# Softplus sum on TensorE, dt*u on VectorE, and three scan inputs in one VectorE instruction

## The reference, cut to what matters

```python
seq = xw.reshape(b, 64, 64).transpose(0, 2, 1)      # 64 steps of one window
x, z = jnp.split(seq @ W_in, 2, axis=-1)            # 128 channels each
x = _silu(conv(x) + conv_b)                         # u
dt, Bm, Cm = jnp.split(x @ W_xproj, [4, 20], axis=-1)
dt = jax.nn.softplus(dt @ W_dt + b_dt)
A = -jnp.exp(A_log)                                 # 128 x 16
def step(h, inp):                                   # h: 128 x 16 states
    h = jnp.exp(dt_t[:, :, None] * A) * h + (dt_t * u_t)[:, :, None] * B_t[:, None, :]
    y = jnp.einsum('bdn,bn->bd', h, C_t)
y = (ys + u * Dp) * _silu(z)
out = y @ W_out
```

## Time and profile before

| | us |
|---|---|
| median of 3 runs (lowest, highest) | 8791.29 (8777.52, 8808.5) |
| the profiled execution | 8805.53 |
| its span in the trace | 8803.7 |
| VectorE busy over the span | 6682.1 (76%) |
| GpSimd busy | 5536.3 (63%) |
| TensorE busy (matmul) | 6314.4 (72%) |
| ScalarE busy | 4408.5 (50%) |
| mean granted clock of TensorE | 0.794 of full speed |

### The profile page before, as it was taken

The page is one execution under the profiler, slowest core; times in us unless marked ns, Lnnn a source line. Parts: engine busy times, 40 slices in busy tenths (PEclk is TensorE's granted clock), DMA queues, the critical chain, the costliest instruction groups (busy, mean ns, idle before and its releaser), DMA issues. The chain is left out here.

```text
span 8803.7 us, 102835 instructions
## 1 busy us (share of the span) xinstructions
PE 6314.4 (72%) x30290; PEld 2534.8 (29%) x30290; DVE 6682.1 (76%) x7810; ACT 4408.5 (50%) x5988; POOL 5536.3 (63%) x2731
## 2 busy tenths in 40 slices
PE   5888888888885767667777766677776766776555
PEld 3444444444442222222222222222222222222133
DVE  3555555555555999999999999999999999999634
ACT  1222222222223766666666666666666667676400
POOL 0000000000004999999999999999999999999600
PEclk8887787787877888887788888887788888788666
DMA  1111111111113555555555555555556555555553
GB/s 30 42 38 42 36 42 38 38 43 36 38 40 115 193 195 198 187 207 185 208 183 205 186 201 194 195 199 192 201 183 210 183 204 186 203 191 197 152 151 128
DMA packets 513971, 1253.45 MB, mean 142 GB/s; under 512 B 170085, under 2 KB 172297, under 8 KB 513673
## 3 DMA queue, kind: packets, MB, share of 16 engines
q1 hardware_dynamic: 513417, 1252.41, 42.2%
q0 software_dynamic: 512, 0.53, 0.0%
HBM read 943.30 MB, written 231.21 MB: 133 GB/s over the span
## 5 line engine op out<-in xcount | busy, mean ns | idle before, releaser
L1177 DVE TENSOR_TENSOR_SCAN b_h<-b_a,b_h 128x448 f32<-128x448 f32 x3584 | 3677.3, 1074 | 294.0 <-POOL b_h L1002 148.2
L1014 POOL TENSOR_TENSOR b_h<-b_h,b_ct 128x896 f32<-128x896 f32 x1792 | 3692.1, 2090 | 24.2 <-DVE b_h L1177 16.6
L1105 ACT ACTIVATE b_a<-b_dts,decay 128x441 f32<-128x441 f32 x3584 | 2227.4, 629 | 1583.9 <-DVE b_h L1177 1564.3
L1264 PE MATMUL b_b<-b_rows,spread_b 16*128 16x512 f32 (+1 forms) x1792 | 697.9, 786 | 1487.5 <-DVE b_h L1167 1486.5
L1025 POOL MEMSET b_seq<- 128x938 f32 x2 | 1.7, 882 | 2645.9 <-POOLq L789 2645.9
L1167 DVE TENSOR_TENSOR b_h<-b_dus,b_b 128x896 f32<-128x896 f32 x1344 | 1432.9, 1066 | 73.7 <-DMA b_dus<-d_dtu 71.3
L490 DVE TENSOR_TENSOR a_xg<-a_xd,a_pb 128x784 f32<-128x784 f32 x512 | 495.3, 967 | 637.7 <-PE a_pb L604 635.5
L1272 PE MATMUL b_y<-b_h,fold 128*32 128x512 f32 (+1 forms) x7168 | 953.7, 659 | 6.8 <-POOL b_h L1014 6.8
L1002 POOL TENSOR_TENSOR b_h<-b_dus,b_bt 128x896 f32<-128x896 f32 x448 | 936.5, 2091 | 10.5 <-DMA b_dus<-d_dtu 10.5
L1264 PEld LDWEIGHTS b_b<-b_rows,spread_b 16*128 16x128 f32 x1792 | 167.4, 228 | 1756.4 <-DVE b_h L1167 1754.7
L1233 PE MATMUL b_w<-b_seq,w_conv 128*128 128x384 f32 (+1 forms) x896 | 540.5, 765 | 12.5 <-DMA b_seq<-b_seq 12.5
(11 more groups left out here) (208 smaller groups left out, 8940.3 us busy)
## 6 DMA issues: line engine op xcount, KB each, us to landing
b_bt<-d_rows SPq DMA_DIRECT2D x448, 448.0 KB, 6.0
b_ct<-d_rows SPq DMA_DIRECT2D x448, 448.0 KB, 3.6
b_dts<-d_dt SPq DMA_DIRECT2D x448, 448.0 KB, 6.0
b_dus<-d_dtu SPq DMA_DIRECT2D x448, 448.0 KB, 6.0
a_xd<-a_xn SPq DMA_DIRECT2D x256, 196.0 KB, 3.4
d_dt<-b_dt SPq DMA_DIRECT2D x112, 448.0 KB, 2.6
d_dtu<-b_soft SPq DMA_DIRECT2D x112, 448.0 KB, 2.5
b_seq<-b_seq SPq DMA_DIRECT2D x112, 234.0 KB, 3.5
```

Source lines behind the costliest of these rows:

```text
L1014: nc.gpsimd.tensor_tensor(hh[t][:], hh[t][:], ct[t // 4 % 2][:], ALU.mult).then_inc(hc_done, 1)
L1105: a(steps(bank(aa, k)), steps(half(dts[t % 4], k)), ACT.Exp, scale=decay[:, t % 4, t // 4:t // 4 + 1]).then_inc(a_done, 1)
L1177: v.tensor_tensor_scan(half(hh[t], k), bank(aa, k), half(hh[t], k), 0.0, ALU.mult, ALU.add).then_inc(h_done, 1)
L1264: last = mm(bb[:, lo:hi], spread_b[q, row, :], rows[i][q, lo:hi], start=True, stop=True)
```

## The change

The sum of softplus leaves POOL. TensorE multiplies `dtb` (relu) and then `soft` (ln) by the identity matrix into `ww`, accumulating; DVE makes `soft` = `ww` * u (`dt_input`, behind the scan of tile 9); ACT copies `ww` into `dtb` (`dt_move`, behind the exps of tile 10). The list has an entry "dt" more, between "xp" and "z". POOL's two products are gone. `softplus_end` is split: Exp at t = 6, Ln at t = 7. `z` moves from t = 10 to 12, the logits from 12 to 14, the tokens from 14 to 15, `residual` from 14 to 15, and POOL's input of the next unit's row 0 from 13 to 14.

The inputs of the three tiles of a row that DVE makes become one instruction of 3 x 896 elements, with `bb` read three times by a stride of zero. It stands at t = 1, 5, 9, 13. `b_done` now counts rows, so TensorE may overwrite `bb` once that one instruction is done. SP stores dt last of the three stores, and loads `dus[1..3]` together behind the input of row 3, ahead of the loads of `dts`.

```diff
-            EVEN = ("xc", "var", "conv", "pre", "xp", "z", "out")
-            ODD = ("xc2", "var2", "conv", "pre", "xp", "z", "lgp", "tok")
+            EVEN = ("xc", "var", "conv", "pre", "xp", "dt", "z", "out")
+            ODD = ("xc2", "var2", "conv", "pre", "xp", "dt", "z", "lgp", "tok")
@@ sync
                             if more:
-                                store_dt(par, o)
                                 sp.wait_ge(moved, spot(i, "xp", it, kind) + 2)
                                 store_rows(par)
                                 store_dtu(par, o)
+                                store_dt(par, spot(i, "dt", it, kind))
...
+                                sp.wait_ge(b_done, row_no(i, 3, it))
+                                for b in range(1, 4):
+                                    load_dus(b, par)
                                 for b in range(4):
                                     sp.wait_ge(a_done, half_no(i, 12 + b, 1, it))
                                     if b == 0:
                                         sp.wait_ge(dt_stored[par], stored)
                                     load_dts(b, par)
-                                    if b:
-                                        sp.wait_ge(b_done, b_no(i, 12 + b, it))
-                                        load_dus(b, par)
@@ gpsimd
-                            nc.gpsimd.tensor_tensor(dtb[:], dtb[:], soft[:], ALU.add).then_inc(dt_ready, 1)
-                            pool.wait_ge(dt_ready, o)
-                            nc.gpsimd.tensor_tensor(soft[:], dtb[:], u[j][:], ALU.mult).then_inc(dtu_ready, 1)
...
-                                if t in (13, 15) and more:
+                                if t in (14, 15) and more:
                                     inputs(1 - i, t // 15, it + i)
@@ scalar
+                        def dt_move(c, o):
+                            act.wait_ge(dtu_ready, o)
+                            move(c, dtb[:])
...
                                 if t == 6 and more:
-                                    softplus_end(o + 1)
+                                    softplus_exp(o + 1)
+                                if t == 7 and more:
+                                    softplus_ln(o + 1)
...
                                 if t == 10 and more:
+                                    dt_move(spot(i, "dt", it, kind), o + 1)
+                                if t == 12 and more:
                                     act.wait_ge(yz_ready, o - 1)
                                     move(spot(i, "z", it, kind), gate[1 - i][:])
-                                if t == 12 and finals:
+                                if t == 14 and finals:
...
-                                if t == 14 and finals:
+                                if t == 15 and finals:
@@ vector
+                        def inputs(row, i, it):
+                            if row == 0:
+                                for b in range(1, 4):
+                                    dve.wait_ge(dus_in[b], 16 * unit_no(i, it))
+                            dve.wait_ge(bt_spread, row_no(i, row, it))
+                            dve.wait_ge(folded, row_no(i, row, it) - 4)
+                            v.tensor_tensor(hh_all[:, 4 * row + 1:4 * row + 4, :], dus_all[:, 1:4, :],
+                                            bb[:, 0:TB].unsqueeze(1).broadcast_to([P, 3, TB]), ALU.mult).then_inc(b_done, 1)
...
+                        def dt_input(c, j, o):
+                            dve.wait_ge(made, c + 2)
+                            v.tensor_tensor(soft[:], ww[:, 0:TB], u[j][:], ALU.mult).then_inc(dtu_ready, 1)
...
-                                if t % 4:
-                                    inputs(t, i, it)
+                                if t % 4 == 1:
+                                    inputs(t // 4, i, it)
...
+                                if t == 10 and not (kind == LAST and i == 1):
+                                    dt_input(spot(i, "dt", it, kind), 1 - i, unit_no(i, it) + 1)
-                                if t == 14 and i == 0 and kind != FIRST:
+                                if t == 15 and i == 0 and kind != FIRST:
@@ tensor
+                        def softplus_sum(c, o):
+                            pe.wait_ge(l_ready, o)
+                            pe.wait_ge(moved, c + 1)
+                            for lo, hi in banks(TB):
+                                mm(ww[:, lo:hi], ident[:], dtb[:, lo:hi], start=True, stop=False)
+                                last = mm(ww[:, lo:hi], ident[:], soft[:, lo:hi], start=False, stop=True)
+                            last.then_inc(made, 1)
...
                             fold_row(0, tile_no(i, 3, it))
                             if more:
+                                softplus_sum(spot(i, "dt", it, kind), unit_no(i, it) + 1)
+                            spread_row(3, i, it)
+                            if more:
                                 gate_in(spot(i, "z", it, kind), 1 - i)
-                            spread_row(3, i, it)
```

More of the change, by code:

```diff
@@ L765, in phase_b @@
                 dts = ring("dts", 4)
-                dus = ring("dus", 4)
+                dus_all = sb("dus", [P, 4, TB])
+                dus = [dus_all[:, n, :] for n in range(4)]
                 bt = ring("bt", 2)
                 ct = ring("ct", 2)
-                hh = ring("h", HH)
+                hh_all = sb("h", [P, HH, TB])
+                hh = [hh_all[:, n, :] for n in range(HH)]
                 aa = psum("b_a", [P, 2 * BANK], F32, st)
@@ L782, in phase_b @@
                 sq_ready, rstd_ready, xn_ready, seq_ready = (sem(n) for n in ("sq", "rstd", "xn", "seq"))
-                abs_ready, e_ready, l_ready, dt_ready, dtu_ready = (sem(n) for n in ("abs", "e", "l", "dt", "dtu"))
+                abs_ready, e_ready, l_ready, dtu_ready = (sem(n) for n in ("abs", "e", "l", "dtu"))
                 skip_ready, yz_ready, gate_ready = (sem(n) for n in ("skip", "yz", "gate"))
                 a_done, h_done = (sem(n, 2 * TILES) for n in ("a", "h"))
-                b_done, hc_done = sem("b", TILES - 8), sem("hc", TILES)
-                pb_done, bt_spread, folded = (sem(n, 8) for n in ("pb", "spread", "fold"))
+                hc_done = sem("hc", TILES)
+                b_done, pb_done, bt_spread, folded = (sem(n, 8) for n in ("b", "pb", "spread", "fold"))
                 sq2_ready, rstd2_ready, xl_ready = (sem(n) for n in ("sq2", "rstd2", "xl"))
@@ L863, in store_rows, with store_dt @@
                             sp.dma_start(rows_d[par, :, :], rows[par][0:2 * NS, :]).then_inc(rows_stored[par], 16)
-                        def store_dt(par, o):
-                            sp.wait_ge(dt_ready, o)
+                        def store_dt(par, c):
+                            sp.wait_ge(moved, c + 2)
                             sp.dma_start(dt_d[par, :, :], dtb[:]).then_inc(dt_stored[par], 16)
@@ L940, in _ @@
                         store_dtu(0, 2)
+                        store_dt(0, START.index("dt"))
                         sp.wait_ge(rows_stored[0], 16)
@@ L1014, in unit @@
                                 nc.gpsimd.tensor_tensor(hh[t][:], hh[t][:], ct[t // 4 % 2][:], ALU.mult).then_inc(hc_done, 1)
-                                if t == 6 and more:
-                                    products(1 - i, unit_no(i, it) + 1)
                                 if t == 4 and i == 0 and kind != LAST:
@@ L1028, in _ @@
                         sequences(None, 1, None)
-                        products(0, 2)
                         inputs(0, 0, 1)
@@ L1144, in _ @@
                         softplus_start(START.index("pre"))
-                        softplus_end(2)
+                        softplus_exp(2)
+                        softplus_ln(2)
                         move(START.index("xp"), rows[0][:], rows=4 * NS)
+                        dt_move(START.index("dt"), 2)
                         act.wait_ge(aa_zero, 1)
@@ L1158, in _ @@
                         v = nc.vector
[L1160 to L1167, removed]
+                        def inputs(row, i, it):
[6 more added lines that the diff above has]
+                                            bb[:, 0:TB].unsqueeze(1).broadcast_to([P, 3, TB]), ALU.mult).then_inc(b_done, 1)
                         def scan(t, i, it):
                             if t % 4:
-                                dve.wait_ge(b_done, b_no(i, t, it))
+                                dve.wait_ge(b_done, row_no(i, t // 4, it))
                             else:
@@ L1259, in spread_row @@
                         def spread_row(row, i, it):
-                            pe.wait_ge(b_done, b_no(i, 4 * row - 1, it) if row else b_no(i, UNIT - 1, it) - (UNIT - 4))
+                            pe.wait_ge(b_done, row_no(i, row, it) - 1)
                             for k, (lo, hi) in enumerate(banks(TB)):
```

14 lines of the change are left out of this document (6 added, 8 removed).

## The result

The change makes the kernel 1.5% faster: 8652.58 us in the median (8637.96 to 8665.33, 4 runs) against 8784.41 (8772.08 to 8808.5, 4 runs), ratio 0.9846 with a 95% interval of 0.9815 to 0.9877. The forecast was 8685. The profiled execution took 8665.33 us, 140 less than that of before. A turn now lasts (7912.1-4057.6)/40 = 96.36 us in place of 98.8; the forecast was 96.8. Of the 32 us between 8685 and 8652.6, 24 are the turns (0.44 x 55) and 7 the median of the kernel before, 8784 here where the forecast started from 8791.

What follows compares the result with a forecast made beforehand. POOL bounds stage B, then DVE: 91.1 + 5.2 (ACT stalls) + 0.5 (TensorE, loads) = 96.8 us per turn, 2.0 less; times 55 turns, +5 at the start, gives -105 us, so 8685 us; 8-in-10 range 8540 to 8850.

Steps and rivals of the forecast that it cites:

- POOL bounds, then DVE: Stage B: POOL bounds the 98.8 us turn; relieved to 90.2, it leaves DVE, at 91.1, as next bound.
- DVE's own 91.1 us: DVE's work per turn after the change: scans 63.2, merged inputs 23.0 and five others at 0.98 us each.
- fixed-part rival: DVE's merged input: each instruction removed saves its whole fixed part, 143 ns; time 8588 us, chance 0.07.
- ACT's stalls, 5.2 us: DVE's scans wait for ACT's extra operations, mainly before tiles 3 and 6: 5.2 us per turn, possibly 2.6 to 7.6.
- The sum: Stage B turn: 91.1 + 5.2 + 0.5 = 96.8 us, 2.0 less than 98.8.
- its own work of 89.7: DVE's work per turn before the change, from start-to-start distances of scans, inputs, gated and residual: 89.7 us.
- TensorE and the loads, 0.5 us: DVE's waits for TensorE's softplus sum and the dus loads together: 0.5 us per turn, bounds 0 and 3.
- late-sum rival: TensorE at the lower clock delivers the softplus sum late to DVE; time 8930 us, chance 0.12.
- The waits on POOL: DVE's 2.7 us per turn for POOL's input and 2.6 before gated are POOL's limit and go once it is relieved.
- the earlier release of B: TensorE's spreading of B and the convolution start earlier, gaining what ACT sometimes waits there; no size given.
- The start: Start of stage B: the chain sum, product, copy replaces two POOL instructions once, about +5 us.
- The range: Whole time, 8 in 10: 8540 (DVE's stalls at half) to 8850 us (softplus sum late by 1.9 us per unit).

Runs made afterwards that it cites:

- e10: Changed kernel plus three spare POOL products per unit with unused output, behind t = 6: 8897.2 us, turn 100.65 us, single run.
- e1: Kernel before plus only the merged three-tile input, its semaphore and the moved dus loads; POOL keeps its products: 8789.3 us, ratio 0.9997.
- e7: Changed kernel plus an unused DVE reduce per unit before scan 3, where DVE waited for ACT: 8662.0 us, single run.
- e8: Changed kernel plus an unused DVE reduce per unit before scan 13, where DVE waits for nothing: 8796.4 us, single run.
- e5: Changed kernel with softplus spread further: Abs at t = 5, Relu at 6, Exp and Ln at 7; 8583.6 us, ratio 0.9772.
- e2: Changed kernel with the old one-by-one inputs, old b_done counting and old place of the dus loads: 8763.6 us, ratio 0.9963 to before.
- e11: Changed kernel with Exp of norms at t = 3, Relu at 6, softplus Exp at 7, z at 11, logits at 12: 8512.5 us, ratio 0.9668.

## Why the prediction was right, step by step

- *POOL bounds, then DVE.* Right. e10 and e1 show POOL's bound from both sides: put back, it sets the turn; left in place, it hides the merged input altogether. The margin was as small as forecast: POOL 90.1, DVE 90.9 before its stalls.
- *DVE's own 91.1 us.* Nearly right: 2.84 us from start to start for the merged input where I took 2.87, so 90.9. The fixed-part rival is out. The Trainium skill's (N+151) cycles ("VectorE: DVE Perf Modes", section on the TRN2 errata) gives 2.96 us for 2688 elements and 1.09 for 896, and the durations are 2.93 and 1.066; the rule holds for the duration within 1 to 2%, but in a full queue a merge of three saves 3 x 0.98 - 2.84 = 0.10 us, not two fixed parts of 0.157.
- *ACT's stalls, 5.2 us.* The mechanism is right and sized within 0.1 us at three of four places: 1.16 for 1.25 before scan 3, 0.82 for 0.91 before scan 6, 0.18 for 0.3 at the logits. The fourth, 0.4 in front of scan 1, occurs in 12 turns of 41, 0.16 per turn: `center` ran at the full clock in 32 of 42 turns (1.77 us at 26.44, where I had 3.35). Total 4.4. e7, e8, e5 support the mechanism: the place decides, not the amount of work.
- *The sum.* The terms as measured, 90.9 + 4.4 + 0.4 = 95.7, leave 0.7 of the 96.36 open. Most of it is in how a wait is counted, from the end of the instruction before; but two instructions in a row overlap by 0.08, and a wait takes that away too. From the starts, scan 3 is 1.22 us late and scan 6 0.92, nearer to the 1.25 and 0.91. With 6 waits per turn this is 0.5, so in the units of the prediction ACT's stalls are about 4.8 to 4.9, 0.3 to 0.4 below the forecast, and that is most of the difference between 96.8 and 96.36. The remaining 0.2 has no owner. The prediction could have seen this gap: its own work of 89.7 and the waits of the earlier trace rows give 97.7 for the turn of 98.8.
- *TensorE and the loads, 0.5 us.* 16.2 us in 41.5 turns, 0.4. The sum was ready in time, with less to spare than I had: it took 5.0 us where 3.5 was assumed, and `dt_input` starts 0.1 us behind it, where 1.7 was the margin. The late-sum rival did not happen, but was near. The dus loads land in 4.9 us in the median, faster than the 6.0 of the earlier trace rows; the loads of dts became the late ones (186 us of ACT's waiting), and DVE is covered by the input of row 0: before the scan of tile 0 it waits once in the 4000 us. That the loads of dts land in 7.4 us in the median where they took 6.0 before was not explained.
- *The waits on POOL.* Here the prediction was wrong in a step, though not in its sum. It counted DVE's 2.6 us before `gated` as POOL's limit. e2 and e1 show that it is TensorE's: input of tile 3, spread of row 1, slow convolution, fold. It stays when POOL is relieved (91.4 us in e2) and goes with the merged input while POOL is full (e1). That the sum held all the same is luck in this step: the change had both edits, but the prediction let POOL's part alone end this wait. I had written that the earlier release of B gains "what ACT sometimes waits there" and gave it no number; in truth, without it, the relief of POOL brings 0.4% instead of 1.5%.
- *The start.* First input at 2763.2 for 2760.6 us, with this stage starting 3.2 us sooner: 5.8 us in all, taken as 5. The reason was only in part the one given. The store of dt*u is issued 1.0 us later within the stage (2745.52 for 2747.66); the rest comes behind it, where the first input now needs three loads in place of one.
- *The range.* Its upper end, 8850, goes by the prediction's own figures with a sum that is 1.7 us late per unit; 1.9 would give 8868. The result does not hang on it.

## What to carry to other kernels

When the bound moves to an engine that was at 92%, look not at its busy share but at what stands between its long runs of instructions: a helper with a one-deep handshake (here two PSUM banks) can do an extra of x only where the leader pauses for x. Merging instructions moves those pauses, so the helper's extras have to move with them; doing that by hand (e11) was worth as much again as the change. And a wait that ends on an engine's result is not that engine's limit until the queue ahead of the result has been read: the slow engine may only have been held by an instruction that stood in front.

## What the runs showed that I had not expected

- Two edits that bring 0 and 0.4% alone bring 1.5% together, since each removes one of two limits of nearly the same length: alone the turns are 98.7 and 98.1.
- A POOL product of two reads of one spare tile of zeros takes 1.68 us, one of two different tiles (896 elements, f32, too) 2.09. Whether the operands or the values make the difference was not tried.
- The softplus sum over four products of 512, 512, 384 and 384 columns changed its speed on the way, 5.0 us in all in one unit, where in e2, one right behind other work, its parts took 1.13, 1.02, 0.81 and 0.81.
